# Graph attention on one core: a third of the softmax transposes leave TensorE and go through DRAM and VectorE, and the scores move ahead of the products with v

## What is computed

```python
h = jnp.maximum(_layernorm(x, axis=-1), 0.0)
q, k, v = (_split_heads(h @ W + b) for W, b in ((Wq, bq), (Wk, bk), (Wv, bv)))
scores = jnp.einsum('bhqd,bhkd->bhqk', q, k) / jnp.sqrt(HD)
scores = scores + beta * adj[:, None, :, :]
scores = jnp.where(adj[:, None, :, :] > 0, scores, -9e15)
probs = jax.nn.softmax(scores, axis=-1)
out = jnp.einsum('bhqk,bhkd->bhqd', probs, v)
return x + merge_heads(out)
```

## Time and profile before

| | before |
|---|---|
| median of 3 runs | 535.08 us |
| profiled execution | 535.0 us |
| its span | 533.1 us |
| TensorE busy | 520.9 us, 98% |
| VectorE busy | 451.9 us, 85% |
| ScalarE busy | 462.3 us, 87% |
| GpSimd busy | 127.3 us, 24% |
| granted TensorE clock, mean | 1.000 of 2.4 GHz |
| queue of DMAs of SyncE | 89616 packets, 74.62 MB, 46.5% of 16 engines |

### The profile page before, as it was taken

The page is one execution under the profiler, slowest core; times in us unless marked ns, Lnnn a source line. Parts: engine busy times, 40 slices in busy tenths (PEclk is TensorE's granted clock), DMA queues, the critical chain, the costliest instruction groups (busy, mean ns, idle before and its releaser), DMA issues.

```text
span 533.1 us, 17434 instructions
## 1 busy us (share of the span) xinstructions
PE 520.9 (98%) x5394; PEld 438.7 (82%) x5394; DVE 451.9 (85%) x2285; ACT 462.3 (87%) x1856; POOL 127.3 (24%) x204
## 2 busy tenths in 40 slices
PE   8989999999999999999999999999999999999995
PEld 8768888888888888888888888888888888888774
DVE  6788998888898898898888889888889987765896
ACT  3558899999999999999999999998998999888984
POOL 4522222212212222221221222222122111101211
PEclk9999999999999999999999999999999999999999
DMA  7523374654646465464645556364565434222111
GB/s 238 186 81 91 115 215 123 201 154 133 192 137 188 123 170 176 123 192 140 189 134 149 177 143 192 128 188 133 138 189 161 128 116 123 71 80 75 51 56 46
DMA packets 89671, 75.25 MB, mean 141 GB/s; under 512 B 39056, under 2 KB 86288, under 8 KB 89616
## 3 DMA queue, kind: packets, MB, share of 16 engines
q1 hardware_dynamic: 89616, 74.62, 46.5%
HBM read 40.37 MB, written 34.21 MB: 140 GB/s over the span
## 4 chain that ended last, share of the span: by engine, by line
PE 90%; DVE 2%; issue 1%; DVEq 0%
PE G_ps L797 35%; PE S_ps L868 18%; PE PT_ps L852 17%; PE S_ps L817 10%; PE PT_ps L834 9%; DVE probsT L682 1%; DVE probs L651 0%; PE G_ps L852 0%; PE PT_ps L858 0%; DVE outT L634 0%; PE S_ps L878 0%; DVE y L701 0%; PE S_ps L894 0%; DVE y L669 0%; DVE qk L621 0%
## 5 line engine op out<-in xcount | busy, mean ns | idle before, releaser
L481 ACT ACTIVATE probs<-probs,negmax 128x128 f32<-128x128 f32 x768 | 298.1, 397 | 0.1
L651 DVE CUSTOM_DVE_ANT_0 probs<-S_ps,bias 128x128 f32<-128x128 f32 x768 | 164.2, 283 | 3.3 <-PE S_ps L817 3.3
L481 ACT ACTIVATION_READ_ACCUMULATOR probs<-probs,negmax 128x1 f32 x768 | 150.2, 196 | 0.0
L452 POOL TENSOR_TENSOR y<-y,x_ring 128x384 f32<-128x384 f32 x63 | 63.4, 1007 | 343.6 <-DVE y L669 343.6
L797 PE MATMUL G_ps<-h_hi,w_lo 128*128 128x512 f32 x288 | 117.7, 409 | 0.0
L797 PE MATMUL G_ps<-h_hi,w_hi 128*128 128x512 f32 x288 | 117.7, 409 | 0.0
L797 PE MATMUL G_ps<-h_lo,w_hi 128*128 128x512 f32 x288 | 116.2, 403 | 0.0
L489 ACT COPY probsT<-PT_ps 128x512 f32<-128x512 f32 x181 | 99.9, 584 | 12.0 <-PE PT_ps L852 11.4
L852 PE MATMUL PT_ps<-ident,probs 128*128 128x128 f32 x728 | 103.6, 277 | 0.0
L852 PEld LDWEIGHTS PT_ps<-ident,probs 128*128 128x128 f32 x728 | 81.9, 141 | 10.3 <-issue 1.0
L868 PE MATMUL S_ps<-w_hi,h_hi 128*128 128x384 f32 x192 | 65.2, 339 | 0.0
(11 more groups left out here) (57 smaller groups left out, 603.6 us busy)
## 6 DMA issues: line engine op xcount, KB each, us to landing
out_dram<-y SPq DMA_DIRECT2D x63, 192.0 KB, 1.9
x_ring<-in_x_dram SPq DMA_DIRECT2D x15, 768.0 KB, 5.4
out_rows<-out_blocks SPq DMA_DIRECT2D x58, 192.0 KB, 1.9
out_moved<-out_rows SPq DMA_DIRECT2D x232, 48.0 KB, 2.1
xhat_rows<-xhat_blocks SPq DMA_DIRECT2D x26, 384.0 KB, 2.6
xhat_moved<-xhat_rows SPq DMA_DIRECT2D x104, 96.0 KB, 2.7
adj_in<-in_adj_dram SPq DMA_DIRECT2D x16, 256.0 KB, 3.2
x_ring<-in_x_dram SPq DMA_DIRECT2D x4, 192.0 KB, 3.2
```

Of the source, the lines that this page charges most:

```text
L452: nc.gpsimd.tensor_tensor(y[:, z.s % 2 ^ d, :], y[:, z.s % 2 ^ d, :], x_ring[:, bass.ds(at, D)], ALU.add).then_inc(y_ready, 1)
L481: last = nc.scalar.activation(p, p, ACT.Exp, bias=negmax[:, e, j * KC + m:j * KC + m + 1], scale=TURN, accum_out=rowsum[:, e, m * HC + j:m ...
L651: last = nc.vector.tensor_tensor_reduce(probs[:, a, j, m, :], S_ps[:, j, m * N:(m + 1) * N], bias[(z.par + 1) % 2][:, z.s, :], 1.0, LARGES ...
```

## The change

1. **The first four heads' probs.** `transpose_probs(z, 0)`, four TensorE transposes, and ScalarE's copy `store_probsT(z, 0)` are gone from the slots of groups 1 to 15. Their four exponentials now run one slot earlier (`exponentials_ahead`: in the slot of the item's own mask, after its last bank) and write `probs_blocks`. SyncE writes that tile to DRAM (`probs_rows`, 256 KB), in the next slot reads it back in four reads of 64 KB (`probs_moved`), and VectorE turns the blocks into `probsT` (a new `transpose_probs(z)` behind `add_bv`).
2. **Order.** In the slots s = 1, 2, 3 TensorE runs `scores` before `probs_times_v` (`scores_first`), and VectorE runs `reciprocals`, two banks of `mask`, `store_outT`, and then the other two banks. In slots s = 0 the products with v stay first. `transpose_blocks` and `normalise` are behind `mask` in all slots.
3. **Units of q and k.** Unit 2 goes from VectorE to ScalarE (STORE_0); VectorE keeps unit 5.
4. **Loads.** A group of x comes in four loads of one item each and not in one; SyncE's slot begins with the reads of `probs_moved`, and the load of adj is in slot 1.
5. **Start.** The four first items of x are loaded ahead of the weights; VectorE does the first `low_part` before the last `normalise`; GpSimd's first splitting of weights waits for VectorE's; in group 0 `low_part` comes earlier in the slot and ScalarE stores unit 5; 22 dummy matmuls in place of 30.
6. **End.** The reciprocals of the last item are one instruction and not three, ScalarE does one of its copies, and in the last slot but one the copies of `probsT` are ahead of the quotient, one of them on ScalarE.

```diff
-STORE_V = [[], [2], [], [5]]
-WARM = [8, 4, 4, 6, 8]
+STORE_0 = [[], [], [2], []]
+STORE_V = [[], [], [], [5]]
+WARM = [8, 2, 2, 3, 7]
...
+        probs_blocks = sb("probs_blocks", [P, HC * FOUR])
+        probs_rows = nc.dram_tensor("probs_rows", [2, P, HC * FOUR], F32, kind="Internal").ap()
+        probs_moved = sb("probs_moved", [P, 2, HC * FOUR])
...
+                self.R = self.E and not self.F
+                self.Q = self.A and self.P and not (n == NG - 1 and s == GROUP - 1)
+                self.scores_first = self.A and self.P and s > 0
...
             def slot(z):
+                if z.R:
+                    sp.wait_ge(probs_rows_written, 16 * (z.e + 1))
+                    for c in range(HC):
+                        came = probs_rows[(z.s - 1) % 2, :, c * FOUR:(c + 1) * FOUR].rearrange("(r p) n -> p r n", r=HC)
+                        goes = probs_moved[c * HD:(c + 1) * HD, (z.s - 1) % 2, :].rearrange("p (r n) -> p r n", r=HC)
+                        sp.dma_start(goes, came).then_inc(probs_blocks_moved[(z.s - 1) % 2], 16)
...
+                if z.Q:
+                    sp.wait_ge(probs_ready[0], z.a + 1)
+                    sp.dma_start(probs_rows[z.s % 2, :, :], probs_blocks[:, :]).then_inc(probs_rows_written, 16)
                 if z.W:
                     sp.wait_ge(out_rows_written, 16 * (z.o + 1))
...
+            def exponentials_ahead(z):
+                act.wait_ge(masked, z.a + 1)
...
+                if started(z.a):
+                    act.wait_ge(probs_rows_written, 16 * z.a)
+                a = z.s % 2
+                blocks = probs_blocks.rearrange("p (c j e) -> p j c e", c=HC, j=HC)
+                for j in range(HC):
+                    last = nc.scalar.activation(blocks[:, j, :, :], probs[:, a, j, 0, :].rearrange("p (c e) -> p c e", c=HC), ACT.Exp,
+                                                bias=negmax[:, a, j * KC:j * KC + 1], scale=TURN, accum_out=rowsum[:, a, j:j + 1])
+                last.then_inc(probs_ready[0], 1)
...
+            def transpose_probs(z):
+                dve.wait_ge(probs_blocks_moved[(z.s - 1) % 2], 64 * (z.moved_before() + 1))
+                if started(z.e):
+                    dve.wait_ge(pv_done, z.e)
+                nc.vector.transpose(probsT[:, 0, :].rearrange("p (j r e) -> p r j e", j=HC, r=HC),
+                                    probs_moved[:, (z.s - 1) % 2, :].rearrange("p (r j e) -> p r j e", r=HC, j=HC)).then_inc(pT_stored[0], 1)
...
+                if z.O and not z.F:
+                    reciprocals(z)
+                if z.O and z.scores_first:
+                    mask(z, [0, 1])
                 if z.O:
                     store_outT(z)
+                if z.O and z.scores_first:
+                    mask(z, [2, 3])
+                elif z.A and not z.F:
+                    mask(z)
                 if z.M:
                     transpose_blocks(z)
...
             def probs_times_v(z):
                 pe.wait_ge(v_stored, z.o + 1)
...
+                pe.wait_ge(pT_stored[0], z.o + 1)
                 pe.wait_ge(pT_stored[2], z.o + 1)
...
+                if z.A and z.scores_first:
+                    scores(z)
                 if z.O:
                     probs_times_v(z)
-                if z.A:
+                if z.A and not z.scores_first:
                     scores(z)
-                if z.E:
-                    transpose_probs(z, 0)
```

196 lines of the change are left out of this document (112 added, 84 removed).

## The result

The changed kernel takes **565.8 us** (median of 4 runs, 564.8 to 567.7) against 535.1 (4 runs, 534.8 to 535.3): a ratio of 1.058, 95% interval 1.055 to 1.061. I had forecast 542.2 us with a range from 531 to 552. The sign was right, the size was not. The profiled execution is the slowest of the four, 567.7 us with a span of 565.5; before, the span is 533.1.

A forecast was written before the change was run, and what follows sets the result against it. TensorE, busy 98%, was taken as the bound before, and the loop through VectorE's list as the bound after in groups 2 to 13. 535.0 + 15.0 - 3.3 - 3.5 - 1.0 = 542.2 us, range 531 to 552.

The forecast's parts named there:

- The order makes the loop long: Groups 2 to 13: VectorE's list between scores makes slots 8.28 or 7.78 us, groups 1.25 us longer; +15.0 us.
- I cost this at nothing: Probs' write and reads through DRAM on SyncE's queue: in time for VectorE's block transpose, cover 0.1 us in the worst slot.
- the late probs: Rival: probs land late, VectorE stands at their block transpose, 1 us in one slot of four, 554 us; chance 0.14.
- the one of the DMA engines in bursts: Rival: DMA engines become the bound, bursts of transfers sticking out 1 us a group, 554 us; chance 0.01.
- The ends, together -3.5 us: Start of the kernel: two early TensorE waits mostly go and the first `project` comes earlier; -3.5 us, from 0 to -6.
- TensorE's part: Four transposes fewer a slot, 0.41 us, so 1.64 us less a group; a gain only where TensorE remains the bound.
- The two groups in which I let TensorE bound: Groups 14 and 15: VectorE's list is shorter, TensorE bounds and gains 2 x 1.64, -3.3 us.
- "The ends" at the finish: End of the kernel: the shorter `last_output` gives -1 us, from 0 to -2.
- no cost; its cover is 1.3 us: ScalarE loses a copy and gains a unit; `h_hi` is ready near 6.3 us and `low_part` wants it at 7.6.
- DMA engines: Over a group: DMA share goes from 0.53 to about 0.72, at most 31.2 us, under the group's 32.6.
- TensorE stays the bound: Rival: the loop closes in 7.43 us or less, 24.2 us come off, 506.3 us; chance 0.08.
- I had left it at 1.00 throughout: Granted clock: taken to stay at 1.00, the level of 2.4 GHz.

The follow-up runs named there:

- e2: The changed kernel, but scores no longer wait for `low_part` except at a group's first slot or where h goes through the scores' banks; 555.7 us.
- e5: The changed kernel with VectorE's block transpose of the probs moved behind `low_part`; 555.7 us.
- e7: The changed kernel with the edits of both e5 and e6; 546.3 us.
- after: The changed kernel itself, against the kernel before at 535.1 us; 565.8 us, ratio 1.058.
- e8: The changed kernel with the write of the probs issued from ScalarE's queue behind its exponentials, not from SyncE's; 559.2 us.
- e15: The changed kernel with x's loads and out's stores issued by GpSimd and not SyncE; 565.3 us.
- e3: The changed kernel with, in group 1 alone, SyncE's write of h's rows moved behind the write of the probs; 559.8 us.
- e12: e9 with the write of the probs issued from ScalarE's queue in place of SyncE's; 543.2 us.
- e9: e7 with scores first in slot 0 too and unit 5 stored by ScalarE; 542.8 us.
- e16: e13 with GpSimd's two small operations for rstd ahead of its DMA issues; 525.6 us, ratio 0.981 to the kernel before.
- e10: e9 with the fill's write of h's rows behind that of the probs, as in e3; 539.0 us.
- e11: The changed kernel with all slots in the old order: products with v first, `transpose_blocks` and `normalise` ahead of the mask; 561.7 us.
- e6: The changed kernel with `transpose_blocks` and `normalise` ahead of the mask again in slots 1 to 3; 553.5 us.
- e13: e10 with x's loads and out's stores issued by GpSimd and not SyncE; 549.0 us.
- e4: The changed kernel with the edits of both e2 and e3; 550.8 us.

## Why the prediction was right or wrong

- **"The order makes the loop long", 8.28 and 7.78 us**: right. Slots with nothing else late take 8.23 and 7.83, e2 takes the loop away and gets TensorE's pace, e5 to e7 shorten it: 0.42 us for 0.64 taken out, 0.35 for 0.82, where `add_bv` then waits for v, and down to TensorE's pace for both. Of the 33.32 us that a group of after takes, this is the part foreseen.
- **"I cost this at nothing" (the probs' way through DRAM, cover 0.1 us in the worst slot)**: this is the step that failed. It let the write leave when the exponentials are done, 5.9 us after the scores, and had no term for the write's landing before the reads may leave; in the slot shown the write left at 7.40 and took 3.93, with the DMA engines 0.98 busy. I gave the late probs a rival of 0.14 with 1 us in one slot of four. In the steady part one slot of four is up to 0.9 us longer than 8.23, 0.48 in the mean, and the border takes a further 0.14, where ScalarE's copy is late; with the rest it is 33.32 - 32.62 = 0.70 a group, 7.0 us over ten. This step's part of the 25.2 us is the 6.1 of e3 and some 4.2 of the 7.0, since e8, with the probs in time, has that slot at 8.29 in place of 8.71. The rival had the right mechanism and slot and twice the size, and the one of the DMA engines in bursts has a part in it. e8 and e15 show that it isn't one wait: with the probs in time, ScalarE's copy or out's quotient is late by as much.
- **"The ends, together -3.5 us"**: wrong by 9.4 us at item 4, and by 16.9 at item 12. I reckoned the cover of the probs from a steady slot and never walked SyncE's queue through groups 1 to 3. In group 1 the write of the probs stands behind h's rows, which wait for a `normalise` in another place on VectorE than later: 6.1 us, shown by e3. I had named the queue ahead of slot 2 (h, adj, two pieces of x), but counted its issues, not its wait. The other 3.3 at item 4 are savings that did not come: in e3 the first scores come 0.95 us earlier than before (27.37 against 28.32), but the four slots from there take 7.27, 8.45, 8.74 and 8.45 us where before they took 7.57, 8.29, 8.29 and 8.05. What the first gives back, the others take again. The 7.5 between items 4 and 12 I can only describe: slots of up to 10.2 us, late transfers of out and of the probs. By item 12, e8 is 8.7 us ahead of after, and e12 is 6.8 ahead of e9, with nothing but the probs' write out of SyncE's queue; e16 is 3.3 ahead of e10 with the stores and loads out of it. So most of this too hangs on that queue. Which of its waits is worth what stays open.
- **"TensorE's part", 1.64 us a group less**: right. A group before has slots of 7.73, 7.96, 7.96 and 7.72; where nothing is late e10 has 7.32, 7.56, 7.56 and, from item 51 to 52, 7.32: 0.40 less in each. The two groups in which I let TensorE bound gave 2.17 us (59.78 against 61.95), not 3.3: group 15 gave 1.60 (28.98 against 30.58), but group 14 only 0.57 (30.80 against 31.37), where TensorE still stands 0.7 us for `low_part` and VectorE once 0.4 for the probs.
- **"The ends" at the finish, -1 us**: -0.8, right.
- **ScalarE, "no cost; its cover is 1.3 us"**: nearly right for the change (0.17 before the products in slot 0), but e11 shows that in the order before ScalarE would have been the bound at 8.13 us. I had not priced the move by itself.
- **DMA engines**: right as to share, 0.70 against 0.72; e16 runs at 0.78, so they did not bound the slower runs over a group. Within it they can be full for some us, 0.98 over the 3.9 us of the write shown.
- **The rival "TensorE stays the bound" (0.08)** needs a version of the change with another order on VectorE, SyncE and GpSimd. e16 comes near it, and gives 525.6 us and not 506.3: its groups take 30.36 and not 29.73, 6.3 us over ten, and its item 12 comes 1.9 us later than before, where this rival has the savings of the start and of three groups.

## What to carry to other kernels

Work taken off the bound engine pays only if every other engine's list, in program order, closes its loop in the shorter slot: here the same instructions in four orders (after, e6, e5, e7) took 8.23, 7.88, 7.81 and 7.56 us in the same slot. A transfer that goes through a shared queue must be walked entry by entry with the waits ahead of it and with its own landing where another waits for it, and in the fill apart from the steady part, because there a wait may stand elsewhere in its engine's list. Moving issues to an idle engine is only free behind that engine's own urgent work (e13 against e16: 23 us).

## What the runs showed of the hardware

- Four reads of 64 KB that were issued in 1.8 us land 2.1 us after issue in the median, and the 256 KB write in 2.8; behind 1024 KB of other transfers issued in the 2 us or so before it, the same write took 3.99 once and 3.93 once before its reads could leave, the second with the DMA engines 0.98 busy.
- A DMA issue mostly takes 0.54 to 0.67 us on GpSimd (e13, e16) and 0.33 to 0.50 on SyncE, and GpSimd stood 0.69 us for its own y before it could issue. x's loads took 3.8 us to land from GpSimd (e13) and 3.3 from SyncE (e10).
- VectorE's block transpose of 128x512 is busy 0.71 us, 0.64 from start to start.
- In the fill TensorE stood idle for 4.73 us, and behind it the granted clock was 0.50, its lower level of 1.2 GHz, from 56.00 to 60.00: 24 of its matmuls took 1.66 us there and 0.95 in the slot before. I had left it at 1.00 throughout. That cost some 1.8 us. Over the whole kernel the clock does not order the runs: the mean of a whole run is 0.99 in after, 1.00 in e3, and 0.98 in e4, which is quicker than both.
